# Edge filters as strip products, gray values through DRAM, and image statistics moved into the attention's first turn

## The reference

```
gray  = einsum('bchw,c->bhw', x, (0.2989, 0.587, 0.114))
edges = conv(gray, scharr, stride 1, padding 'SAME')      # two 3x3 filters
h     = (|edges[0]| + |edges[1]|) / 2                     # 8 x 256 x 256
h     = concatenate([h, txt], axis=1)                     # 8 x 384 x 256
h     = h + attention0(layernorm(h))    # 16 heads of 16, two softmaxes (keys K and K')
h     = h + fp4_feed_forward(layernorm(h)); then attention and 8 experts of layer 1
```

## Time and profile before

| | |
|---|---|
| time, median of 3 | 1815.2 us |
| profiled execution, time | 1817.46 us |
| its span | 1815.7 us |
| granted TensorE clock, mean | 0.988 of 2.4 GHz |
| busy: PE, DVE, ACT, POOL | 1747.6, 1005.1, 677.3, 409.7 us |
| DMA over the span | 112.84 MB, mean 62 GB/s |

### The profile page before, as it was taken

How to read it: one execution, slowest core, us unless ns; L and a number is a source line. 1 busy time by engine, 2 the same in 40 slices (tenths; PEclk the granted TensorE clock), 3 DMA queues, 4 the chain that set the end, 5 groups by cost and what they waited for, 6 DMA issues and landing times.

```text
span 1815.7 us, 29086 instructions
## 1 busy us (share of the span) xinstructions
PE 1747.6 (96%) x9935; PEld 1115.4 (61%) x9935; DVE 1005.1 (55%) x2073; ACT 677.3 (37%) x1290; POOL 409.7 (23%) x415
## 2 busy tenths in 40 slices
PE   7989999899999998999999999999999999999997
PEld 3324444344444435777755666666767679999997
DVE  6597877778788898888865444443211112222221
ACT  2106656566666686545532322233010111111110
POOL 2101120110201003898722221110211211000000
PEclk9988999999999999999999999999999999999999
DMA  6832632426324402000074000000000003423211
GB/s 190 138 66 41 119 78 43 82 45 114 74 47 87 82 2 74 1 0 0 1 294 110 0 0 0 1 1 1 34 28 20 32 20 111 175 104 107 102 32 34
DMA packets 111955, 112.84 MB, mean 62 GB/s; under 512 B 11455, under 2 KB 104433, under 8 KB 111858
## 3 DMA queue, kind: packets, MB, share of 16 engines
q1 hardware_dynamic: 98610, 83.21, 20.3%
q10 hardware_dynamic: 9600, 18.92, 2.9%
q0 software_dynamic: 3648, 9.46, 1.4%
HBM read 78.51 MB, written 32.93 MB: 61 GB/s over the span
## 4 chain that ended last, share of the span: by engine, by line
PE 88%; DVE 7%; issue 2%; ACT 2%; DMA 0%; DVEq 0%; POOL 0%; ACTq 0%; POOLq 0%
PE ps_e L2218 11%; PE ps_e L2151 9%; PE ps_a L614 8%; PE ps_a L588 7%; PE ps_m L1651 6%; PE ps_a L603 6%; PE ps_e L2227 5%; PE ps_m L1794 5%; PE ps_e L2160 5%; PE ps_m L1722 4%; PE ps_m L1752 4%; PE ps_a L559 4%; PE ps_m L1667 3%; DVE mx L961 3%; PE ps_a L688 2%
## 5 line engine op out<-in xcount | busy, mean ns | idle before, releaser
L961 DVE TENSOR_REDUCE mx<-ps_a 128x1 f32<-128x384 f32 x768 | 379.7, 550 | 52.2 <-PE ps_a L588 50.4
L820 ACT ACTIVATE prob<-ps_a 128x768 f32<-128x768 f32 (+1 forms) x512 | 305.7, 650 | 96.7 <-PE ps_a L603 95.7
L588 PE MATMUL ps_a<-w,qs 96*128 96x384 bf16 x768 | 242.1, 338 | 7.7 <-DVE mx L961 3.8
L603 PE MATMUL ps_a<-qs,w 100*128 100x384 bf16 x768 | 207.1, 331 | 5.5 <-issue 4.0
L2218 PEld LDWEIGHTS ps_e<-xTr,w 128*128 128x128 f32 x1792 | 206.0, 193 | 2.2 <-issue 0.8
L2218 PE MATMUL ps_e<-xTr,w 128*128 128x128 f32 x1792 | 206.3, 276 | 0.6 <-DVE xTr L2394 0.6
L588 PEld LDWEIGHTS ps_a<-w,qs 96*128 96x128 bf16 x768 | 72.9, 98 | 182.2 <-DVE mx L961 103.6
L614 PE MATMUL ps_a<-prob,vp 128*32 128x384 f32 x1536 | 163.3, 498 | 0.0
L2151 PE MATMUL ps_e<-xT_all,w 128*128 x448 | 145.7, 486 | 0.0
L2283 ACT ACTIVATE gel_r<-ps_e 128x512 f32<-128x512 f32 x56 | 33.4, 597 | 280.9 <-PE ps_e L2218 280.9
L1651 PE MATMUL ps_m<-w 128*128 128x352 f32 x384 | 122.3, 462 | 2.2 <-ACT w L1828 1.2
(11 more groups left out here) (266 smaller groups left out, 2585.1 us busy)
## 6 DMA issues: line engine op xcount, KB each, us to landing
w<-parts_dram SPq DMA_DIRECT2D x192, 96.0 KB, 5.2
w<-in_L_ffn_W_dram ACTq DMA_DIRECT2D x18, 1024.0 KB, 8.3
parts_dram<-w SPq DMA_DIRECT2D x24, 576.0 KB, 3.4
qs<-parts_dram SPq DMA_DIRECT2D x96, 96.0 KB, 4.0
prob<-in_x_dram SPq DMA_DIRECT2D x24, 256.0 KB, 3.6
w<-in_L_ffn_W_dram SPq DMA_DIRECT2D x6, 1024.0 KB, 12.8
grouped_x<-empty_row SPq DMA_DIRECT2D x1, 4352.0 KB, 24.3
grouped_h<-empty_row SPq DMA_DIRECT2D x1, 4240.5 KB, 33.9
```

The costliest lines, as they stand in the source:

```text
L588: mm = pe.matmul(ps[:, r % 3, 0:T], qs[0:NS, b, u // 2, t * P:(t + 1) * P], ks[0:NS, b, u % 2, u // 2], start=True, stop=True)
L603: mm = pe.matmul(ps[:, scores_at(v, more) + t, 0:T], ks[0:NS + 4, b, kp, hh, t * P:(t + 1) * P], qs[0:NS + 4, b, hh], start=True, stop=True)
L820: act.activation(prob[:, g % 2, j, ts.start:ts.stop], ps[:, at + ts.start:at + ts.stop, 0:T], ACT.Exp).then_inc(exp_done.sem, 1)
L961: dve.tensor_reduce(at, ps[:, r % 3, 0:T], AX.X, ALU.max).then_inc(ring_free.sem, 1)
```

## The change

The edge filter is written as products of strips. An image is cut into 8 strips of 32 rows; with a row above and below each has 34. The operand of a product is `im`: 34 rows for each of three horizontal shifts, 102 partitions in all, and the band matrix is 102 x 32 (`band`, `masks`). A filter of an image is 8 products of 256 columns, four of them side by side in the four column groups of the array; there are no corner products and no side rows. To build `im`, the gray image goes to DRAM (`gray_dram`, with a border of zeros) and comes back as 3 copies of 34 x 8 x 256. The taps come as 3 copies of 34 rows, one for each part of `im`.

Gray values of images 4 to 7 are made by ScalarE (three scalings) and GpSimd (two sums); images 0 to 3 stay on VectorE. The sum of the two filters stays on VectorE for images 0 and 1 and moves to GpSimd for images 2 to 7. Statistics of images 3 to 7 move into the first turn, units 22 to 26, with one root in unit 28 on ScalarE and one reciprocal in unit 30. Edges of image 0 come behind the turning of the weights, edges 1 and 2 behind the projections of image 0, edges 3 to 7 whole in ring steps 6, 16, 20, 24 and 28.

```diff
-    TAPS = [(f, kx) for f in range(2) for kx in range(4)]
-    BESIDE = 6
+    LATER = 22
+    STRIP = 32
+    HALO = STRIP + 2
+    ROWS = 3 * HALO
+    STRIPS = IMG // STRIP
+    PAD = IMG + 2
+    BY_DVE = 4
+    CONV_AT = {6: 3, 16: 4, 20: 5, 24: 6, 28: 7}
...
+            def store_gray(i):
+                if i < BY_DVE:
+                    sp.wait_ge(gray_step.sem, gray_step.at(i + 1, 0))
+                else:
+                    sp.wait_ge(summed.sem, summed.at(i + 1 - BY_DVE, 0))
+                sp.dma_start(gray_dram[i, 1:IMG + 1].rearrange("(a p) n -> p a n", p=P), grays[:, i]
+                             ).then_inc(gray_out[i % 2].sem, 16)
+            def strips(i):
+                sp.wait_ge(row_out.sem, 32)
+                sp.wait_ge(gray_out[i % 2].sem, gray_out[i % 2].at(i // 2 + 1, 0))
+                if i >= 2:
+                    sp.wait_ge(edges_done.sem, edges_done.at(i - 1, 0))
+                for kx in range(3):
+                    corner = gray_dram[i, 0:1, kx:kx + 1]
+                    rows = bass.AP(corner.tensor, corner.offset, [[PAD, HALO], [STRIP * PAD, STRIPS], [1, IMG]])
+                    sp.dma_start(im[kx * HALO:(kx + 1) * HALO, i % 2], rows).then_inc(im_in[i % 2].sem, 16)
-            sp.dma_start(taps[:], scharr.rearrange("f o a b -> (f o a b)").partition_broadcast(P)
-                         .rearrange("p (f a b) -> p f a b", f=2, a=3)).then_inc(taps_in.sem, 16)
+            for kx in range(3):
+                sp.dma_start(taps[kx * HALO:(kx + 1) * HALO].rearrange("p f a -> p (f a)"),
+                             scharr.rearrange("f o a b -> b (f o a)")[kx].partition_broadcast(HALO),
+                             allow_slow_non_contiguous=True).then_inc(taps_in.sem, 16)
...
+            def edge_rows(i):
+                pool.wait_ge(mag_done.sem, mag_done.at(i, 2))
+                pool.tensor_tensor(h[:, i * TT:i * TT + 2], mag[:, i % 2, 0], mag[:, i % 2, 1], ALU.add).then_inc(h_later.sem, 1)
+            def sum_gray(i):
+                j, g = i - BY_DVE, gray_of(i)
+                pool.wait_ge(scaled_done.sem, scaled_done.at(j, 2))
+                pool.wait_ge(borders.sem, 2)
+                pool.tensor_tensor(g, pix[:, i % 2, 0], pix[:, i % 2, 1], ALU.add).then_inc(summed.sem, 1)
...
+            def edges(i):
+                u = i % 2
+                pe.wait_ge(im_in[u].sem, im_in[u].at(i // 2 + 1, 0))
...
+                for f in range(2):
+                    for a in range(2):
+                        for c in range(STRIPS // 2):
+                            mm = pe.matmul(ps[c * STRIP:(c + 1) * STRIP, 4 + 2 * u + f, a * IMG:(a + 1) * IMG], band[0:ROWS, f],
+                                           im[0:ROWS, u, a * (STRIPS // 2) + c], start=True, stop=True, tile_position=(0, c * STRIP))
+                    mm.then_inc(edges_done.sem, 1)
...
+                    if not prev and v == LATER + B - 2:
+                        roots(3, B)
...
+                    if not prev and LATER <= v < LATER + B - 3:
+                        moments(v - LATER + 3)
+                    if not prev and v == LATER + B:
+                        inverses(3, 3, B)
```

More of the change, by code:

```diff
@@ L261, in attention0 @@
         kind_rows = sb("kind_rows", [4, KINDS, T], BF16)
-        taps = sb("taps", [P, 2, 3, 3])
+        taps = sb("taps", [P, 2, 3])
+        band = sb("band", [P, 2, STRIP])
+        masks = sb("masks", [P, 3, STRIP])
         ps = ctx.enter_context(nc.psum_tensor("ps_a0", [P, 8, 512], F32))
@@ L447, in _ @@
                          .rearrange("p a b -> p (a b)")).then_inc(alpha_in.sem, 16)
+            image(2)
+            store_gray(1)
+            image(3)
+            strips(1)
+            store_gray(2)
             def kinds(b):
@@ L451, in kinds @@
                                  ).then_inc(ks_ready[b].sem, 16)
-            for i in range(2, B):
-                image(i)
             sp.wait_ge(kinds_made.sem, 4)
             kinds(0)
+            strips(2)
+            store_gray(3)
             store_parts(0)
             stacks(0, 0, 0)
+            image(4)
+            strips(3)
+            image(5)
             stacks(0, 0, 1)
-            sp.wait_ge(edges_done.sem, edges_done.at(BESIDE, 0))
+            for i in range(4, B):
+                store_gray(i)
+                if i + 2 < B:
+                    image(i + 2)
+                strips(i)
             kinds(1)
@@ L704, in turn_weight @@
                 mm.then_inc(wTd.sem, 1)
-            pe.wait_ge(corner_in.sem, 32)
-            for n in range(len(TAPS)):
-                edges(0, n)
             pe.wait_ge(ident_done.sem, 1)
@@ L712, in _ @@
                 turn_weight(n)
-            for n in range(len(TAPS)):
-                edges(1, n)
+            edges(0)
             pe.wait_ge(wTe.sem, 5)
@@ L723, in _ @@
                 freed.append((signal, n + 1))
-            for i in range(2, BESIDE):
-                for n in range(len(TAPS)):
-                    edges(i, n)
+            edges(1)
+            edges(2)
             pe.wait_ge(rest_done.sem, rest_done.at(0, 3 * KC))
@@ L850, in roots @@
                 act.activation(rstd[:, tiles], mv[:, tiles, 1], ACT.Sqrt, bias=eps[:]).then_inc(root_done.sem, 1)
[L852 to L865 removed]
+            act.wait_ge(borders.sem, 1)
+            act.activation(rstd[:, 0:1], eps[:], ACT.Sqrt, bias=eps[:]).then_inc(root_done.sem, 1)
             for n in range(5):
@@ L1140, in _ @@
+                n += 1
+                for ky in (1, 2):
+                    dve.wait_ge(bands_done.sem, n)
+                    dve.scalar_tensor_tensor(to, masks[0:ROWS, ky], taps[0:ROWS, f, ky:ky + 1], to, ALU.mult, ALU.add
+                                             ).then_inc(bands_done.sem, 1)
+                    n += 1
+            dve.wait_ge(borders.sem, 2)
+            make_gray(0)
             edge_rows(0)
@@ L1164, in _ @@
                     low_parts(1, PREPARE[r][1])
[L1165 to L1173 removed]
+            inverses(2, 2, 3)
             for_images(dve, turn)
```

238 lines of the change are left out of this document (98 added, 140 removed).

## The result

The changed kernel takes 1942.9 us, the median of 4 runs (1941.5 to 1944.0); the kernel before takes 1815.5 (1815.2 to 1818.1) beside it. The ratio is 1.070, with a 95% interval of 1.068 to 1.072. It is slower by 127 us; the forecast was 1954, from 1925 to 2030.

A forecast was written before the change was run, and what follows sets the result against it. TensorE was taken to bound the preparation's second half, VectorE the round of maxima. First turn at about 270 against 138.2 (+132), plus 7 in it: +139 on 1817.5, 1956.5; less 2.3 for the median, 1954; range 1925 to 2030.

The forecast's parts named there:

- The two engines: Strip copies: 34 leading rows run on two DMA engines at 47 ns a row, 19.2 us an image; chance 0.85.
- The rival at the kind rows' rate: Strip copies: two engines at 0.105 to 0.13 us a row, +190 or +270, about 2145 or 2225 us; chance 0.06.
- The cycle: Late images' strips: 19.2 + 0.8 for the next store + 2.5 from landing to next first packet, 22.5 us an image.
- The taps: Start of the preparation: 612 small pieces, 306 an engine, take 12 us ahead of image 0.
- The tail: SP's queue behind the last strips: kind rows 4, parts 5, waiting and issue 1, stacks 12, maxima's rows 1; ends at 270.
- The turn: First turn: statistics on VectorE +5, root's table change and back on ScalarE 2, together +7 us.
- The first rival: Strip copies: all sixteen engines share them, first turn starts 11 us earlier, 1811 us, between 1803 and 1820; chance 0.09.
- The signs: Expected evidence: DMA share near 0.12 through most of 30 to 245 us, TensorE waiting longest for strips, products 2.2 to 4.5 us.

The follow-up runs named there:

- e1: The changed kernel with each 34-row strip copy issued as one copy of 32 rows and one of 2; 1840.8 us, ratio 1.011 to the kernel before.
- e4: The changed kernel with each 34-row strip copy issued as two copies of 17 rows; 2084.4 us, one run.
- e2: The changed kernel with statistics, root and reciprocal of images 3 to 7 moved from the first turn back to the round of maxima; 1934.5 us, ratio 1.064.
- e7: e1 with statistics, root and reciprocal of images 3 to 7 back in the round of maxima; 1832.5 us, ratio 1.008.
- e13: e7 with each image's 32 strip products, for images 3 to 7, spread over four ring steps, eight after each; 1830.9 us, ratio 1.007.
- e6: e1 with SyncE's list in another order and the statistics of images 3 to 7 back in the round of maxima; 1835.1 us, ratio 1.010.
- e10: e1 with gray values of images 4 and 5 made sooner, SyncE's list following, and statistics back in the round of maxima; 1831.4 us, ratio 1.007.
- e14: e10 with each image's strip products, for images 3 to 7, spread over four ring steps, eight after each; 1833.3 us, ratio 1.008.
- e3: e2 with one root of a single column added in unit 28 of the first turn; 1935.7 us, ratio 1.065.

## Why the prediction was right

**The two engines.** The step on which it stood, 34 leading rows on two engines at whole-row speed, held: share 0.14, 46 GB/s, and e1 and e4 show that the number of leading rows is what decides. The rival at the kind rows' rate is out. The Trainium skill's rule ("DMA: Bandwidth & Descriptors", section "Why a DMA increments its semaphore by 16 and not by 1"), the largest number of engines up to 16 that divides the slowest dimension, gave it before any trace of 34 rows was there; with 17, 32 and 34 rows these runs agree with it.

The row cost 44.5 ns and not 47. That it would be near 47 was a choice more than a reading: the forecast says that every busy window of whole rows moves at that rate, but the stacks' window in the earlier trace rows has 151 GB/s at a share of 1.16, which is 8.1 GB/s an engine and not 21.8. The choice came out; nothing in the rows had decided it.

**Where the 12 us came from.** The first scores came at 258.3 and not at 270. The strips of image 0 were in 4.6 us ahead of the forecast, those of images 1 to 4 3.3 to 4.6, and those of image 7 6.9 (240.6 against 247.5); the tail behind them took 17.7 us and not 22.5, which is the other 4.8. The cheaper row is worth 1 us an image, 8 in all, but it shows only in the last three images.

**The cycle.** From one image's strips to the next I had 22.5 us; the issues stand 22.7, 21.1 and 21.0 apart (154.19, 176.88, 197.99, 219.03). It is built as I had it: image 4's strips are in at 176.05, the next go out 0.8 us later, and they are in 20.3 us after that, 18.2 for the rows and 2.1 around them. SyncE's stall, which I had not foreseen, adds nothing to it: the store whose issue took 5.98 us lands only 0.8 us after the strips ahead of it.

**The taps.** The term was too large. I gave them 12 us and put image 0 at 17 us. VectorE used the taps at 9.2 and image 0 had landed at 11.8. The 612 small pieces held the images up little: VectorE begins with image 0 at 11.9 us and not at 6.8 as before, and 2.3 of these 5.1 us are the later issue of its load. With this the strips of image 0 were in at 42.1 us instead of 46.7.

**The tail.** Kind rows, parts, stacks and maxima's rows did stand behind the last strips in SyncE's list, and the round's end (its last maxima at 249.2 against 258 forecast) was not the last to arrive. The order was right. The length was not: the kind rows and the parts went out while image 7's strips were still landing, and I had put the whole tail behind them.

**The turn.** Forecast +7 and measured +6.9 (71.4 to 78.3 us), and that they agree so well is luck: the statistics were put at 5 and cost 6.4, the table switch at 2 and cost 2.8, and 2.8 us go the other way, since e2, with neither in the turn, has a shorter rest than the kernel before (1674.7 against 1677.5). What shortens it was not tested. In the table the three shortest rests (e2, e7 and e13, 1674.7 to 1676.4) are those of kernels with early moments in which 7 to 9.5 us pass between the ring's end and the first scores; where the scores follow at once (e6, e10, e14), the rest is 1678.0 to 1679.1, no shorter than before. The 1.4 us of drain for each switch that the Trainium skill gives ("ScalarE: Activation LUTs", section "What ACT_TABLE_LOAD costs") is not seen in e3: the root costs 2.8 us behind the first scores (1.2 in the medians), and its loads and itself are already 2.9.

**The first rival was wrong in two terms.** With all sixteen engines it had the turn start at 127 us, 11 earlier than before, and 1811 in the end. e1 has it at 155.1, 16.9 later than before, and 1840.8. It put the start of the round at 61 us, and it is 73.7: image 0's way through DRAM, for which this rival had nothing, puts its normalizing at 35.06 us (27.29 before), and the stores of its parts go out at 52.09 (45.03 before):

```profile
35.06 1.07 DVE w L982 x3
...
52.09 7.17 DMA parts_dram<-w
...
67.39 6.19 DMA w<-parts_dram
```

And it put 66 us from there to the first scores, which take 81.4. It had not weighed that TensorE would run in large part at its lower level (0.67 in the mean of 73.7 to 155.1 us, 0.87 in the round before), nor the wait for the maxima's rows, nor that strips cost bytes: 3 x 34 x 8 KB = 816 KB an image beside the 768 KB of its load, at a DMA share of 0.76 through the same window:

```profile
73.70:155.10 81.40, 61.07 (x289) 21.69 (x290) 50.97 (x110) 15.99 (x30) 24.37 (x25) 0.67 0.76 164
```

So even without the 34 rows the change would have lost. I had 0.05 for faster; this case deserved less.

**The signs.** Two DMA engines, the strips as TensorE's longest wait and 3.5 to 3.6 us for an image's products came as named. That the DMA share would be near 0.12 through most of 30 to 245 us did not: it is so in about half of that time, in the rest loads and stacks run beside the strips.

## What to carry to other kernels

Look at the leading dimension of each copy before its bytes: 34 rows went out at 46 GB/s and 32 + 2 rows at 213, and that one number was 102 of 127 us (the 213 include the start of an image's load). Work taken off a busy engine pays only if what replaces it keeps the engine fed; here 36 us less of TensorE in the preparation became waiting, and then matmuls at the lower clock. Statistics "moved to where there is room" need that room counted on the chain of waits: in the stretch they moved to there was 1.4 us for 6.4.

## What the runs showed of the hardware that I had not expected

- The issuing engine stalls behind a copy with few engines. With 34 rows three issues took 8.3 to 12.5 us, with 17 rows six took 26.6 (image 0), with 32 + 2 rows six took 2.1 to 3.1 (e1). All that stands behind on SyncE waits too. It is not only few engines that do this: twelve issues of the stacks took 9.1 us in e1 at 79.8, behind strips and an image load on all engines, and 5.6 at 62.2.
- A copy over all sixteen engines lands late behind two loaded ones: the gray store of image 7 took 12.5 us in the changed kernel and at most 5.8 in e1 (issued at 122.7, landed before the strips go out at 128.5); that of image 0, ahead of all strips, took 5.2. That it waits for its slowest engine is my reading of it.
- TensorE, busy 20.00 of 20.00 us by the profile's rows with 102x32 and 96x128 weights (e13), was granted 0.50 throughout. The kernel before had 0.71 with 16.18 of 19.00 busy in the same place.
